# Each engine's own table of side steps for the routing that runs beside the experts

## The reference

```python
x = x + 0.5 * ffn(layernorm(x))     # mixture of experts
x = x + attention(layernorm(x))     # 16 heads of 8, full softmax
x = x + 0.5 * ffn(layernorm(x))     # the same experts again

def ffn(x):
    scores = softmax(x @ gate_w.T)                 # 8 experts
    sel = top_k(scores + expert_bias, 2)           # 2 for each row
    # rows are scaled by their score, sorted by expert, and for each expert e:
    #   h = silu(xe @ w1[e]) * (xe @ w3[e]);  out = h @ w2[e]     (128 -> 352 -> 128)
    # and each row's two results are added up
```

## Time and profile before

| | |
|---|---|
| three timed runs | 844.72, 844.98, 851.7 us (median 844.98) |
| the profiled execution | 854.1 us, of which 852.3 us from the first to the last instruction |
| TensorE busy | 651.6 us, 76% of the span |
| VectorE, ScalarE, GpSimd busy | 437.5, 395.2, 302.3 us |
| first expert stage, loads 0 to 45 | from about 61 us to 247 us |
| second expert stage | from about 592 us to 797 us |

### The profile page before, as it was taken

One profiled execution on the slowest core, in us unless ns is written; L12 is line 12 of the kernel. 1 busy time (PEld: TensorE's weight loads), 2 busy tenths in 40 slices (PEclk: granted clock), 3 DMA queues, 4 the chain that ended last, 5 costly groups with the idle time before them and its releaser, 6 DMA issues.

```text
span 852.3 us, 14693 instructions
## 1 busy us (share of the span) xinstructions
PE 651.6 (76%) x4966; PEld 483.1 (57%) x4966; DVE 437.5 (51%) x1115; ACT 395.2 (46%) x926; POOL 302.3 (35%) x311
## 2 busy tenths in 40 slices
PE   4237999999987378887988999676798899889500
PEld 4236888888963134444544554335687788679400
DVE  3724572222345667977988888671457122123211
ACT  0333572433431157756867787583267234234200
POOL 4026543566313243034000000103654345554474
PEclk9999999999995569999989999865899889899855
DMA  6154795777826334244423432015379567567422
GB/s 227 37 182 108 220 265 171 221 204 208 241 88 194 106 99 133 89 131 139 132 88 120 126 107 90 2 57 165 102 216 253 158 187 205 162 194 220 132 77 62
DMA packets 114747, 126.03 MB, mean 148 GB/s; under 512 B 12464, under 2 KB 96944, under 8 KB 114416
## 3 DMA queue, kind: packets, MB, share of 16 engines
q1 hardware_dynamic: 88688, 98.05, 38.2%
q0 software_dynamic: 9088, 18.63, 9.0%
q10 hardware_dynamic: 16896, 8.39, 3.3%
HBM read 89.37 MB, written 35.39 MB: 146 GB/s over the span
## 4 chain that ended last, share of the span: by engine, by line
PE 51%; DVE 19%; issue 10%; ACT 7%; POOL 5%; DMA 3%; another core or an unknown queue 3%; SPq 1%; ACTq 0%; DVEq 0%; POOLq 0%
PE banks L624 10%; PE banks L602 7%; PE banks L607 7%; PE banks L612 7%; DVE mx L917 6%; PE banks L823 6%; POOL rows L541 3%; ACT PT L837 3%; PE banks L753 2%; PE banks L592 2%; PE banks L796 2%; PE banks L462 2%; PE banks L442 2%; ACT oT L890 1%
## 5 line engine op out<-in xcount | busy, mean ns | idle before, releaser
L521 POOL DMA_INDIRECT xe<-routed_rows,idx x156 | 151.7, 972 | 214.9 <-DMA routed_rows<-xn 77.0
L917 DVE TENSOR_REDUCE mx<-banks 128x2 f32<-128x512 f32 x256 | 163.0, 685 | 26.0 <-PE banks L798 20.0
L541 POOL DMA_INDIRECT rows<-slots_out,slot x128 | 123.2, 962 | 106.2 <-ACT PT L837 33.0
L837 ACT ACTIVATE PT<-banks 128x512 f32<-128x512 f32 x256 | 140.3, 602 | 43.3 <-PE banks L809 36.0
L675 DVE TENSOR_TENSOR hidT<-banks,act 96x256 f32<-96x256 f32 (+1 forms) x92 | 34.9, 380 | 237.4 <-ACT act L657 173.0
L624 PE MATMUL banks<-WR,hidT 128*128 128x128 f32 x936 | 121.1, 277 | 5.1 <-ACT ye L665 4.3
L624 PEld LDWEIGHTS banks<-WR,hidT 128*128 128x128 f32 x936 | 113.2, 193 | 8.6 <-issue 6.5
L602 PE MATMUL banks<-xeT,WR 128*128 128x256 f32 (+1 forms) x368 | 93.0, 377 | 22.0 <-issue 20.4
L492 POOL TENSOR_TENSOR rough<-var,half_power 128x16 f32<-128x16 f32 (+1 forms) x8 | 18.4, 2296 | 220.4 <-DVE var L258 220.4
L607 PE MATMUL banks<-xeT,WR 128*96 128x256 f32 (+1 forms) x368 | 89.2, 367 | 6.3 <-DVE hidT L675 6.3
L612 PE MATMUL banks<-xeT,WR 128*128 128x256 f32 (+1 forms) x368 | 87.2, 361 | 0.0
(11 more groups left out here) (155 smaller groups left out, 851.0 us busy)
## 6 DMA issues: line engine op xcount, KB each, us to landing
WR<-in_experts SPq DMA_DIRECT2D x92, 544.0 KB
stacks<-split SPq DMA_DIRECT2D x32, 384.0 KB
slots_out<-ye SPq DMA_DIRECT2D x156, 64.0 KB
routed_rows<-xn ACTq DMA_DIRECT2D x32, 256.0 KB
QS<-stacks SPq DMA_DIRECT2D x64, 112.0 KB
KS<-stacks SPq DMA_DIRECT2D x64, 112.0 KB
xe<-routed_rows,idx POOLq DMA_INDIRECT x156
rows<-in_xt SPq DMA_DIRECT2D x2, 1024.0 KB, 9.4
```

The lines of the kernel that those rows point to most:

```text
L521: eng.indirect_dma_start(xe[:, i % XR, a, :], None, routed_rows[h], bass.IndirectOffsetOnAxis(ap=idx[h][:, tile:tile + 1], axis=0))\
L541: eng.indirect_dma_start(rows[:, k, t, :], None, slots_out[h], bass.IndirectOffsetOnAxis(ap=slot[h][:, k, t:t + 1], axis=0))\
L837: eng.activation(PT[:, u % 4, 1 - k].rearrange("p t n -> p (t n)"), PS[f % 3], ACT.Exp, scale=scale).then_inc(s_exp2, 1)
L917: eng.tensor_reduce(mx[:, :, e, pair], MAXIMA[f % 3][:, :].rearrange("p (q n) -> p q n", q=2), AX.X, ALU.max).then_inc(s_max, 1)
```

## The change

In both stages the rule "five ticks in every load of the first group" gives way to a table for each engine: how many ticks stand behind load 0, 1, 2 and so on of the group. The sums (80, 70, 74) are those of the ticks, so all routing is still issued in the first group's loads.

```diff
-        def early(g):
-
-            return lambda i: 5 if g * NL <= i < (g + 1) * NL else 0
+        VECTOR = (3, 3, 1, 2, 13, 3, 3, 3, 15, 3, 3, 3, 2, 1, 1, 1, 19, 0, 1)
+        SCALAR = (0, 0, 0, 0, 17, 0, 0, 0, 0, 24, 3, 4, 3, 3, 4, 3, 3, 4, 2)
+        TENSOR = (0, 0, 0, 0, 0, 0, 0, 0, 39, 0, 0, 0, 0, 0, 0, 0, 33, 2)
+
+        def by_load(g, table):
+
+            return lambda i: table[i - g * NL] if 0 <= i - g * NL < len(table) else 0
...
-            expert_scalar(act, 0, HALVES * NL, (route_scalar(act, 1), early(0), NL - 2))
+            expert_scalar(act, 0, HALVES * NL, (route_scalar(act, 1), by_load(0, SCALAR), NL - 2))
...
-            expert_tensor(pe, 0, HALVES * NL, (route_tensor(pe, 1), early(0), NL - 2))
+            expert_tensor(pe, 0, HALVES * NL, (route_tensor(pe, 1), by_load(0, TENSOR), NL - 2))
```

More of the change, by code:

```diff
@@ L1111, in _ @@
                 pass
-            expert_scalar(act, HALVES * NL, 2 * HALVES * NL, (route_scalar(act, 3), early(2), 3 * NL - 2))
+            expert_scalar(act, HALVES * NL, 2 * HALVES * NL, (route_scalar(act, 3), by_load(2, SCALAR), 3 * NL - 2))
         @block.tensor
@@ L1138, in _ @@
             pe.wait_ge(s_lge, BATCH + 2)
-            expert_tensor(pe, HALVES * NL, 2 * HALVES * NL, (route_tensor(pe, 3), early(2), 3 * NL - 2))
+            expert_tensor(pe, HALVES * NL, 2 * HALVES * NL, (route_tensor(pe, 3), by_load(2, TENSOR), 3 * NL - 2))
         @block.vector
@@ L1154, in _ @@
             expert_vector(dve, 0, HALVES * NL,
-                          (chained(route_norm(dve, 1, 1), route_vector(dve, 1, 1)), early(0), NL - 2),
+                          (chained(route_norm(dve, 1, 1), route_vector(dve, 1, 1)), by_load(0, VECTOR), NL - 2),
                           (done, late(1, 2, 15, 21, 22), -1))
@@ L1168, in _ @@
             expert_vector(dve, HALVES * NL, 2 * HALVES * NL,
-                          (chained(route_norm(dve, 7, 1), route_vector(dve, 3, 1)), early(2), 3 * NL - 2),
+                          (chained(route_norm(dve, 7, 1), route_vector(dve, 3, 1)), by_load(2, VECTOR), 3 * NL - 2),
                           (done, late(3, 1, 12, 17, 22), -1))
```

## The result

The kernel after takes 870.7 us (median of 4 runs, 868.95 to 875.19) against 845.8 us for the kernel before beside it (844.72 to 851.7): ratio 1.029, 95% interval 1.022 to 1.035. It is slower, 36 us above the forecast of 834.8 and outside its range of 823 to 852. The profiled execution took 869.1 us, with a span of 867.3; before it was 854.1 and 852.3. So the two profiles differ by 15.0 us and the two medians by 24.9, because the profiled execution of before was 8 us above its median.

The account below looks back on a forecast made before the run. TensorE was taken to bound the expert stages' loads 3 to 22, with 10 and 15 us to win. Terms -3.6 + 2.0 - 1.6 - 2.6 - 4.4 = -10.2 us, from 845.0 to 834.8 us; range 823 to 852.

Parts of the forecast that it names:

- The square root: VectorE, load 1: root read in load 3, so its wait for GpSimd's power and TensorE's idle times go; -3.6 us.
- The exponential: ScalarE, moved from load 3 to load 4: load 5, a single, then takes 4.3 us; +2.0 us, bounds 0 to +4.
- The scaled copies: ScalarE: three or four per load in loads 9 to 18 instead of five; -1.6 us, bounds -0.2 to -2.6.
- The one-hot rows: VectorE, load 11: five steps spread over loads 12 to 15, ending TensorE's wait for the product behind them; -2.6 us.
- The inversion: TensorE, load 14: 32 small matmuls halved into loads 16 and 17, so the clock stays at 2.4 GHz; -4.4 us.
- GpSimd's next group: Row numbers come in load 18, not 15; load 23's rows still in time with 1.7 us of slack; price 0.
- The rival by which it would fall behind each half: Clock falls behind each half of the inversion: 4.4 us not won and as much lost again; 844 us, chance 0.14.
- GpSimd catches up in one go, and TensorE stands meanwhile: GpSimd sends some 25 gathers in a row per stage while TensorE idles; +11 to +23 us, 854 us, chance 0.12.
- Load 23's rows come late: Rows land 5 us later than the prologue's, TensorE waits 3.5 us a stage; 847 us, chance 0.09.
- the waits only move: Weights and queues bound the expert loads, so a third of the sum is left; 841.5 us, chance 0.15.

Follow-up runs that it names:

- chip F: Chip on which the unchanged kernel after was measured again: 786.2 us against 803.0 for the kernel before.
- e3_third: Kernel after with GpSimd's plain DMAs in place of the expert rows' gathers by index (other rows, wrong output): 802.4 us against 878.2 for the kernel after.
- e1b_held: Kernel before plus one wait holding GpSimd's next-half gathers until 22 loads of the stage are turned: 872.9 us against 846.4 for the kernel before.
- chips B and D: Two chips on which the unchanged kernel after ran again: 874.2 and 878.2 us against 846.4 and 850.6 for the kernel before.
- the first kind: Chips where the kernel before takes 846 to 851 us, as in the result; on the second kind it takes 802 to 804 us.
- before_again: The kernel before, unchanged, run again for its trace: 843.4 us.
- after_fourth: The kernel after, unchanged, run again: 786.2 us against 803.0 for the kernel before on the same chip.
- e3_again: Kernel after with GpSimd's plain DMAs in place of the expert rows' gathers by index (wrong output): 782.5 us against 803.8 for the kernel before.
- chip C: Chip of the second batch to show the faster kernel before, 803.8 us; the kernel after with plain DMAs took 782.5 us there.

## Why the prediction was wrong

By its own steps, in the trace of after unless another is named:

- *The square root*, -3.6: right. Load 3 lost 2.87 us in the first stage before (6.35 against 3.48) and nothing now; in the second 1.24 (4.72) became 0.26 (3.74).
- *The exponential*, +2.0: its mechanism is right, its size only where nothing disturbs it. On chip F load 5 takes 4.41 us, forecast 4.3. In the result load 5 takes 7.29 and load 6, at a clock that fell, 5.23 against 3.48. Loads 4 to 6 lose 5.7 us more than before in the first stage and 1.9 in the second, +7.6 and beyond the bounds of 0 to +4. The place stands beside GpSimd's power and eight gathers in a row, where before there were the power and six; that these are the cause is not shown by a run of its own, but e3_third has the same tables and takes 4.41 us for load 5 in both stages.
- *The scaled copies*, -1.6: right, and more than that. Over loads 7 to 12 the time above full speed falls from 2.4 us to 0.7 in each stage, with 0.4 and 0.5 more in loads 13 to 15: -2.4 in all, near the end of its bounds.
- *The one-hot rows*, -2.6: right. Load 13 took 5.67 and 5.68 us and takes 4.11 and 4.49.
- *The inversion*, -4.4: right to a tenth. Before, loads 14 and 15 lost 4.67 + 1.70 and 4.68 + 2.67 us; now loads 16 and 17 lose 2.35 + 2.34 and 2.35 + 2.38, so 4.3 us less. The clock stayed up. The rival by which it would fall behind each half did not happen. The rule that the prediction weighed for that rival, from the Trainium skill ("TensorE: Matmul & The Clock Gate", A second HAM failure mode), did not decide here: the granted clock was 1.00 across both halves in both stages.
- *GpSimd's next group*, 0: **this is the step that failed.** Its own question, whether load 23's rows are in time, I answered rightly: the last scaled row is issued 4.8 us into load 18 (146.09), as worked out, and GpSimd restarts 4.9 us later and not 6.2, at 151.01. The profile puts no wait to a transpose of load 23; on chip F, where nothing else stalls, load 22 with these transposes takes 4.23 us, as in the trace of before. But what the restart does to TensorE beside it was priced at nothing in the sum, and it cost 15.8 + 18.0 = 33.8 us. Forecast and result lie 35.1 us apart as differences (-10.2 against +24.9), so this one term is nearly all of the miss.

The rival *GpSimd catches up in one go, and TensorE stands meanwhile* had this very mechanism, and went wrong in its price and its chance. I took 0.3 to 0.6 us for each gather from runs of 5 and 7; the table above shows 0.9 to 1.1 us for each in runs of 17 to 23, where the loss is nearly the whole length of the run. The larger of the two rows showed it: at 682.26 TensorE idled 4.17 us behind seven gathers, and loads 17 and 18 together lost 6.9 us (675.00 to 688.23, 13.2 us against 6.4), 1.0 for each. I read the idle time of one row where the lengths of the loads tell the loss. And I gave it 0.12 because the row named no releaser; e1b_held and e3_third together show that it was the cause. *Load 23's rows come late* and *the waits only move* did not happen: loads 3 to 21 gained 3.5 and 11.0 us, more than the sum, since what loads 17 and 18 lost before (1.7 and 6.9 us) went too.

The sum of the two traces: loads 3 to 21 give 14.5 us, loads 22 to 24 take 33.8, the stretch between the last load of one stage and the first of the next, which the change doesn't touch and which takes 344 to 350 us from trace to trace, happens to give 4.7 (348.8 to 344.1 us), and the remaining loads and the two ends take the last 0.4, to the +15.0 of the spans.

## What to carry to other kernels

Releasing a queue later is not free when the rows are still in time: ask how long its owner will then run without a pause, and look in the trace of before for its longest run and for what the loads beside it lost, whole loads and not one idle time. A stall that names no releaser, or that names an engine which was itself waiting for the stalled one, is a reason to look at what runs in parallel and to double it in an experiment: one wait in the old kernel (e1b_held) settled what the comparison of two versions could not. And a difference between two versions can have the other sign on another chip, +3% and -2% here; compare on more than one before keeping either.

## What was unexpected of the hardware

In the result and on chips B and D, gathers by index that GpSimd sends in a row at 1.26 us each hold TensorE up for almost the length of the run. TensorE's matmuls are then signalled late (the twelve at 158.19 only at 175.10), with no wait for a DMA in TensorE's rows and the DMA engines at half their rate of before in the same loads (123 GB/s against 226). On chip F runs of 53 and 67 cost nothing. Plain DMAs of GpSimd with the same bytes cost nothing on either kind.

The same seems to hold for the combining gathers. On the first kind the part between the stages takes 344 to 350 us, on the second 325 to 330. From its start to the 65th activation of L837 it takes 122.8 us in before_again and 109.9 in after_fourth, and runs of 15 and 6 gathers stand there, in after_fourth of 13 and 12; from the 177th to the 256th, where GpSimd sends none, it takes 82.6 us in both. The whole part is 17 us shorter in after_fourth than in before_again (344.4 and 327.2 us) and 21 us shorter in e3_again than in e3_third. That may be nearly half of the 43 us by which the kernel before differs between the kinds, of which the second has no trace. It agrees with e3_third, which has no gathers by index in the expert stages but the combining ones as before: 348.0 us between the stages, and 19.9 us in all above the 782.5 of chip C. No run took the combining gathers out, so for them it is argued and not shown.

What happens within TensorE stays open. The Trainium skill says in "SBUF — State Buffer" (Who interferes with whom) that a DMA never contends with a compute engine. For plain DMAs e3_third agrees (12.4 us for loads 22 to 24 at 268 GB/s); for gathers by index no run tells whether the transfer or GpSimd's work for it is what TensorE feels, only that it loses 15 to 20 us where 17 to 19 stand in a row. Whether pauses in such a run would help was not measured on a chip of the first kind.
